# First attention: two full-height matmuls with a constant operand ahead of every row-maximum tile

## The reference

```python
scores = jnp.einsum('bhqd,bhkd->bhqk', q, k)
scores = scores + jnp.einsum('bhqd,qkd->bhqk', q, rel_pos)
scores = scores / np.sqrt(HEAD_DIM).astype(np.float32)
attn = jax.nn.softmax(scores, axis=-1)
local_ctx = jnp.einsum('bhqk,bhkd->bhqd', attn, v)
```

## Time and profile before

| | |
|---|---|
| median of 3 runs | 4047.76 us (4047.39 to 4051.94) |
| profiled execution, its own time | 4043.93 us |
| profiled execution, span of the trace | 4041.2 us |
| mean granted TensorE clock in it | 0.87 |
| first attention, first to last matmul | 123.2 to about 812.4 us |
| busy in the whole span: PE, DVE, ACT, POOL | 3229.5, 2296.0, 2100.1, 1069.5 us |

### The profile page before, as it was taken

The page is one execution under the profiler, slowest core; times in us unless marked ns, Lnnn a source line. Parts: engine busy times, 40 slices in busy tenths (PEclk is TensorE's granted clock), DMA queues, the critical chain, the costliest instruction groups (busy, mean ns, idle before and its releaser), DMA issues. The chain is left out here.

```text
span 4041.2 us, 71890 instructions
## 1 busy us (share of the span) xinstructions
PE 3229.5 (80%) x23909; PEld 1685.1 (42%) x23909; DVE 2296.0 (57%) x3463; ACT 2100.1 (52%) x3805; POOL 1069.5 (26%) x967
## 2 busy tenths in 40 slices
PE   2578788724960499997399999999999999999997
PEld 1213223111330133332166556556556655655654
DVE  6677677755232477776655545555554554555553
ACT  1355555511210166665166666666666666666664
POOL 0000000001420211111255435434444533543541
PEclk6576666756985599999699999999999999999998
DMA  5222212222428111111311111111111111111111
GB/s 187 68 48 52 63 36 52 48 57 51 107 53 44 24 24 24 28 27 42 100 42 49 32 45 50 31 47 39 46 43 38 49 32 45 53 32 44 39 39 38
DMA packets 192098, 198.89 MB, mean 49 GB/s; under 512 B 114369, under 2 KB 121145, under 8 KB 186970
## 3 DMA queue, kind: packets, MB, share of 16 engines
q1 hardware_dynamic: 154396, 192.23, 18.7%
q10 hardware_dynamic: 37344, 1.97, 1.0%
HBM read 98.98 MB, written 28.81 MB: 32 GB/s over the span
## 5 line engine op out<-in xcount | busy, mean ns | idle before, releaser
L2376 POOL TENSOR_TENSOR tr_t<-tr_t 128x512 f32<-128x512 f32 x384 | 489.0, 1273 | 707.3 <-DVE tr_t L2220 707.3
L2383 POOL TENSOR_TENSOR tr_nq<-tr_t,tr_rn 128x512 f32<-128x512 f32 x384 | 392.6, 1044 | 401.7 <-ACT tr_rn L2116 401.7
L1595 DVE TENSOR_REDUCE attn_mp<-attn_ps 128x1 f32<-128x512 f32 (+3 forms) x660 | 395.5, 657 | 161.8 <-PE attn_ps L1446 86.5
L2081 ACT ACTIVATE tr_pr<-tr_ps 128x768 f32<-128x768 f32 x264 | 213.9, 810 | 385.0 <-PE tr_ps L1903 383.9
L2219 DVE TENSOR_TENSOR tr_t<-tr_ps,tr_tab 128x512 f32<-128x512 f32 x384 | 263.6, 686 | 243.2 <-ACT tr_sq L2090 243.2
L678 DVE TENSOR_REDUCE attn_mcol<-attn_ps 128x1 f32<-128x1024 f32 x274 | 333.2, 1222 | 116.3 <-PE attn_ps L526 115.4
L1918 PE MATMUL tr_ps<-tr_w,tr_xs 128*128 128x512 f32 x768 | 371.2, 605 | 29.1 <-DVE tr_xs L2247 24.7
L2229 DVE TENSOR_TENSOR tr_o<-tr_ps,tr_rd 128x384 f32<-128x384 f32 (+1 forms) x264 | 144.1, 546 | 438.9 <-ACT tr_rd L2106 438.0
L1557 ACT ACTIVATE attn_pr<-attn_ps 128x768 f32<-128x768 f32 (+2 forms) x352 | 300.9, 870 | 166.8 <-PE attn_ps L1479 163.8
L663 ACT ACTIVATE attn_pr<-attn_ps 128x512 f32<-128x512 f32 x512 | 279.6, 597 | 206.9 <-DVE attn_ps L692 200.1
L1903 PE MATMUL tr_ps<-tr_qT,tr_kT 64*128 64x96 f32 (+1 forms) x4224 | 300.8, 282 | 0.0
(11 more groups left out here) (259 smaller groups left out, 5185.1 us busy)
## 6 DMA issues: line engine op xcount, KB each, us to landing
tr_v<-tr_va SPq DMA_DIRECT2D x144, 192.0 KB, 2.5
attn_ka<-scratch_kp SPq DMA_DIRECT2D x72, 288.0 KB, 6.1
tr_v<-tr_va SPq DMA_DIRECT2D x144, 128.0 KB, 2.5
moe_cb<-scratch_combineT SPq DMA_DIRECT2D x32, 512.0 KB
tr_w<-in_w_half SPq DMA_DIRECT2D x12, 1024.0 KB
tr_v<-tr_va SPq DMA_DIRECT2D x48, 256.0 KB, 2.4
scratch_kp<-proj_parts SPq DMA_DIRECT2D x36, 256.0 KB
attn_qg<-scratch_qp SPq DMA_DIRECT2D x10, 784.0 KB
```

What stands on the lines that cost most here:

```text
L1595: dve.tensor_reduce(dst, src, AX.X, ALU.max).then_inc(maxed, 1)
L2376: pool.tensor_tensor(t12[:, slot, i, 0, :], t12[:, slot, i, 0, :], t12[:, slot, i, 1, :], ALU.add).then_inc(summed, 1)
L2383: pool.tensor_tensor(nq[:, slot, i, :].rearrange("p (h e) -> p h e", e=DH), t12[:, slot, i, 0, :].rearrange("p (h e) -> p h e", e=DH), rn[ ...
```

## The change

A tile `warm` of 128 x 512 bf16 is added and set to 1.0 once by GpSimd, ahead of its other memset. In `max_tile`, after all waits of the tile, two matmuls with `warm` as both operands are put ahead of the two score matmuls. They run over all 128 rows and 512 columns and write the same two banks, which the score matmuls then overwrite (`start=True`). TensorE waits for the memset once at the start.

```diff
+        warm = st.sb("warm", [P, CH], BF16)
...
+            pool.memset(warm[:], 1.0).then_inc(zeroed, 1)
             pool.memset(vh[:], 0.0).then_inc(zeroed, 1)
-            pool.wait_ge(zeroed, 1)
+            pool.wait_ge(zeroed, 2)
...
                 if m == TILES:
                     pe.wait_ge(q_loaded[1 - s], 32 * ((g - s) // 2 + 1 + s))
+                for c in range(2):
+                    pe.matmul(ps[:, MAXB + 2 * (pos % 2) + c, :], warm[:, 0:P], warm[:], start=True, stop=True)
                 for c in range(2):
                     mm = pe.matmul(ps[:, MAXB + 2 * (pos % 2) + c, :],
                                    qg[score_rows[c], buf, head % GH, u * P:(u + 1) * P],
...
             pe.wait_ge(consts, 16 * NCONST)
+            pe.wait_ge(zeroed, 2)
```

## The result

The changed kernel is slower: 4137.51 us median of 4 runs (4131.16 to 4138.77) beside 4048.94 us (4047.39 to 4051.94). The ratio is 1.0217, with a 95% interval of 1.0201 to 1.0233. That is 88.6 us more, where +3 was forecast, and it lies outside the range on record. The profiled span is 4135.7 us, 94.5 more than before.

The account below looks back on a forecast made before the run. Windows steps were read as a ring of TensorE matmuls and ScalarE copies, pair phases as TensorE, VectorE and ScalarE taking turns. Terms -44 + 24 + 11 + 10 + 1.6 + 1, about +3, gave 4051 us; range 4022 to 4078.

Parts of the forecast that it names:

- The memset and the lead: Start of the kernel: GpSimd's new memset hidden, 0; opening maxima slowed only until the clock rises, +1 us.
- About half of those empty places should drop the clock for some 7 us: Windows phases: TensorE's waits at turns lower the clock for three to four steps at 0.46 us, 6 us in all.
- rival 3: Windows phases: clock falls back and stays, 15 of 24 steps cost 0.46 us, +28 instead of +6; 4073 us, chance 0.14.
- The price of a windows step: Windows phases at the lower clock: 0.77 + 0.88 + 0.44 = 2.09 us of TensorE, 0.5 us late in each step.
- hidden, 0: Windows step at the higher clock: 1.42 us of TensorE before the next windows, due at 1.57, so no cost.
- The turns (5 us): Windows phases: 8 turns put the tile behind a wait that holds everything, 0.6 us each.
- The term on the path in the pair phases: Pair phases at the higher clock: 3.5 of ten tiles a pair pay 0.43 us, 1.5 us a pair, +24 us.
- step 3: Step of a pair, 3.12 us at the higher clock, forecast to take 3.5 us with the new matmuls.
- Rival 2: Pair phases: everything behind the tile is late, seven of ten tiles pay 0.43 us, 48 us; 4075 us, chance 0.15.
- The clock's gain in the pair phases: Pair phases: the higher clock shortens steps where TensorE is in the chain, -44 us, bounds 0 and -55.
- relapses: Pair phases: lower clock at phase starts, behind turns and at a few pair boundaries, ten at about 1 us, +10 us.
- Wrong if the windows phases stay below 0.7: Sign to check: the clock should exceed 0.9 in the lead's second half, windows and pair phases.

Follow-up runs that it names:

- e9: Changed kernel with six full-height matmuls instead of two ahead of the three tiles behind each of two turns per windows phase; 4110.7 us.
- e3: Changed kernel with one new full-height matmul ahead of each tile instead of two; 4086.07 us, 1.0092 of before.
- e4: Changed kernel with its two new matmuls over 50 rows each instead of all 128; 4042.22 us, 0.9981 of before.
- e5: Changed kernel with the new matmuls over 50 rows each and only ahead of the pair phases' tiles; 4033.09 us, 0.9963 of before.
- e6: As e5, but without the new matmuls ahead of the tiles of the code's steps 1 and 2 of each pair; 4041.29 us.
- e8: Changed kernel with the full-height matmuls only ahead of the tiles of the code's steps 4, 5 and 7 of each pair; 4050.49 us.
- e10: As e5, but without the new matmuls ahead of the tile of the code's step 1 of each pair; 4030.28 us.

## Why the prediction was wrong

- **The memset and the lead** came as forecast: nothing, and +1.5 us for +1.
- **The step that failed is "About half of those empty places should drop the clock for some 7 us", three to four steps at 0.46.** In three of the four windows phases the clock did fall at an empty place, the 1.20 us behind the first turn; in the third it was down before the phase began. But it did not come back after 7 us; it stayed at 0.50 for 49 us and more, to the end of the phase. The 7 us were read off a pair phase, whose steps bring the clock up again. In a windows step two full-height matmuls held the higher level for a time (e9, 162 to 183 us at 1.00) and did not restore it (154 to 203 us at 0.50 in the changed kernel). This is rival 3's mechanism, "falls back in the windows phases and stays". It was given 0.14, and its price was too small: 15 steps of 24 at 0.46, +28, where 21 to 24 at 0.69 make 60.
- **The price of a windows step was under-sized** from 2.09 to 2.27 us: 0.90 for 0.77, 0.97 for 0.88. And "hidden, 0" at the higher clock was wrong by a little, 1.64 against 1.57: the ring then also is TensorE's. The prediction added streaming times and left out some 0.1 us at each place where matmuls over all rows meet narrower ones. Whether that is their weight loads, as e3's expectation had it, no run took apart. The turns (5 us) were not checked one by one.
- **The term on the path in the pair phases was about half of what it is.** "3.5 x 0.43" a pair, +24 us, came out as 2.9 us a pair at the higher clock, or 46 us. The new matmuls cost 0.58 us there. The tiles that it named, those of the code's steps 2, 3 and 5, stand in columns 0, 1 and 3 and do pay; so do columns 2 and 6, which it had counted as free but for a part. The "step 3" for which it forecast 3.5 us took 3.73. Rival 2 had this size, 48 us, for "more than four and a half tiles a pair". The step behind a turn takes 8.5 to 8.6 us for 6.4 to 6.8 and adds 7.8 us, for which 1.6 stood.
- **A misreading without weight.** It took the steps with two tiles for those that gain less from the clock. The step of 3.12 us, which gains 0.99, is itself one with two tiles: the trace has four score matmuls of `max_tile` between its two weighs.
- **The clock's gain in the pair phases was right in mechanism and about in size.** -44 us was forecast; 2.8 us a pair, if the clock stood at 1.00 throughout, is 45. At the clock measured, the lower level covers some 95 us of the pair phases (e.g. 2 x 0.10 x 130 in the first) instead of 276, and 181 x the forecast's own 0.2 is 36 us of gain. Against it stand 46 us on the path, so +10 for the ordinary steps, where +7.5 was measured, and 7.8 us at the turns. For "relapses" it had +10 us; the one such place that can be read by itself are the openings of the phases, which cost 8.5 us: the clock is still down from the windows phase when they begin, and the new pairs in them have the lower clock's price. The matmuls need not be full height for this: e4 and e5 reach 0.81 to 0.90 with half-height ones.
- **Sum.** Windows +62 for +11, pair phases +24 for -8, lead +1.5 for +1. "Wrong if the windows phases stay below 0.7" was the right thing to look at, and it was so.

What stays open is what makes the clock fall. It fell at the first turn of three windows phases of the changed kernel, and ahead of the third phase with no turn there. In the first windows phase of e9 it fell at the first turn and not at the second, which has the same wait of 1.20 us ahead of its tile.

## What to carry to other kernels

Work that is added to hold TensorE's clock pays only where TensorE idles behind it or where it runs beside what is there: the same columns cost 0.58 us over all rows and 0.02 us over rows that let two matmuls run side by side, in the step of the earlier trace rows (0.2 to 0.3 us over the whole of columns 1 and 2). Price it at the lower clock too, for the stretch in which the clock might not hold, and don't take the time of recovery from another phase; the steps of the pair phases restored the level here, those of the windows phases at best kept it. Leave it out of phases in which TensorE waits for another engine at the lower clock already: the windows phases took 41.5 to 43.3 us at 0.50 before, and 48 us or more with one or more full-height matmuls a tile, at any clock. And when an edit goes by the code's step numbers, look in the trace for the place where the instructions come to stand: e6, e8 and e10 changed other steps than the ones that had been measured.

## What the runs showed of the hardware

- The same instructions ran at either level for a long stretch, according to what had gone before: windows steps with two full-height matmuls at 0.50 for 49 us in the changed kernel, at 1.00 for 21 us in e9 (162 to 183 us).
- The busy share of TensorE's records did not tell the level. At 0.50 stood stretches with 35 of 42 us, 41.44 of 44 (e4) and 53.28 of 59 (the changed kernel's third windows phase); at 0.87 one with 95.10 of 122 (e5).
- Two full-height bf16 matmuls of 512 columns take 0.54 us to the next, narrower matmul at the higher level and 0.97 us at the lower one. Two over 50 rows at different places of the array take 0.23 us (e5, 285.82 to 286.05).
- In the pair phases two of eight steps without extra work (e6, the two at the pair boundary) were enough to lose most of what the clock had gained: 0.77 in the first of them, for 0.87 in e5 and 0.74 before.
